# Feed-forward of a transformer layer: the chosen path's mask is read back from DRAM by broadcasting loads instead of being spread by TensorE products

## The reference, cut to what matters

```python
x_mixed = _mix(x, mix_kernel)                       # each row with its two neighbours
h = jnp.einsum('bsd,pdm->bspm', x_mixed, W1) + b1   # 9 paths, 64 hidden values each
stacked_paths = jnp.einsum('bspm,pmd->bspd', h, W2) + b2
scores = jnp.tanh(x_mixed @ Wo1 + bo1) @ Wo2 + bo2
idx = jnp.argmax(scores, axis=-1)
weights = jax.nn.one_hot(idx, P, dtype=stacked_paths.dtype)
collapsed = jnp.einsum('bspd,bsp->bsd', stacked_paths, weights)
return _layernorm(x + collapsed, gamma, beta)       # and x + this, normalised once more
```

## Time and profile before

| | |
|---|---|
| median of 3 runs | 1554.53 us (1553.85 to 1555.71) |
| the profiled execution | 1557.27 us, of which the span of the trace is 1555.6 us |
| feed-forward stage in the trace | from 1181.6 us to the end |
| busy over the whole span | PE 94%, DVE 71%, ACT 62%, POOL 29% |
| granted TensorE clock over the span | 0.97 of full speed |

### The profile page before, as it was taken

One profiled execution on the slowest core, in us unless ns is written; L12 is line 12 of the kernel. 1 busy time (PEld: TensorE's weight loads), 2 busy tenths in 40 slices (PEclk: granted clock), 3 DMA queues, 4 the chain that ended last, 5 costly groups with the idle time before them and its releaser, 6 DMA issues. The chain is left out here.

```text
span 1555.6 us, 25379 instructions
## 1 busy us (share of the span) xinstructions
PE 1458.1 (94%) x8282; PEld 661.4 (43%) x8282; DVE 1104.5 (71%) x2645; ACT 957.7 (62%) x2103; POOL 445.2 (29%) x565
## 2 busy tenths in 40 slices
PE   5979978999999999999999999999988999999995
PEld 3645641333333333333333333333323656666664
DVE  3212239788888888888888888888733788788775
ACT  3635630777777777777777777777775455555432
POOL 5423430211113313213224124124234152222212
PEclk9989985999999999999999999999999999999997
DMA  4887864032364483383383373473632821110001
GB/s 121 267 272 259 270 222 99 26 97 61 101 149 82 118 167 88 111 163 98 110 148 116 118 134 108 126 138 92 118 45 64 151 68 55 55 48 20 28 27 41
DMA packets 166753, 178.19 MB, mean 115 GB/s; under 512 B 26397, under 2 KB 135784, under 8 KB 166632
## 3 DMA queue, kind: packets, MB, share of 16 engines
q1 hardware_dynamic: 166632, 176.70, 44.0%
HBM read 109.79 MB, written 66.06 MB: 113 GB/s over the span
## 5 line engine op out<-in xcount | busy, mean ns | idle before, releaser
L761 ACT ACTIVATE a_probs<-a_ps_s 128x512 f32<-128x512 f32 (+3 forms) x1536 | 648.1, 501 | 232.1 <-PE a_ps_s L934 228.5
L789 DVE CUSTOM_DVE_ANT_0 h_space<-a_ps_m,a_causal 128x640 f32<-128x640 f32 (+5 forms) x768 | 652.5, 888 | 121.1 <-PE a_ps_m L857 107.4
L934 PE MATMUL a_ps_s<-s_qs,s_ks 99*128 99x512 bf16 (+3 forms) x1536 | 406.0, 329 | 6.3 <-ACT a_probs L761 4.5
L857 PE MATMUL a_ps_m<-s_ks,s_qs 96*128 96x512 bf16 (+3 forms) x1536 | 385.9, 338 | 22.5 <-DVE a_mx L789 8.0
L716 POOL TENSOR_SCALAR_AFFINE_SELECT a_probs<-a_probs 128x512 f32<-128x512 f32 x256 | 163.2, 637 | 662.6 <-ACT a_probs L761 662.6
L892 PE MATMUL a_ps_o<-a_probs,s_vq 128*32 128x512 f32 (+3 forms) x3072 | 328.1, 498 | 5.7 <-POOL a_probs L716 3.7
L934 PEld LDWEIGHTS a_ps_s<-s_qs,s_ks 99*128 99x128 bf16 x1536 | 137.2, 97 | 331.0 <-ACT a_probs L761 241.9
L857 PEld LDWEIGHTS a_ps_m<-s_ks,s_qs 96*128 96x128 bf16 x1536 | 130.0, 99 | 201.9 <-DVE a_mx L789 69.3
L226 DVE TENSOR_TENSOR p_rest<-p_ps_qk,h_space 128x512 f32<-128x512 f32 x64 | 44.3, 692 | 154.8 <-ACT h_space L251 154.8
L1403 PE MATMUL f_ps_o<-f_w,f_hm 128*128 128x256 f32 (+1 forms) x640 | 151.1, 384 | 0.9 <-DVE f_y L1310 0.9
L1403 PEld LDWEIGHTS f_ps_o<-f_w,f_hm 128*128 128x128 f32 (+1 forms) x640 | 121.4, 192 | 27.4 <-issue 8.4
(11 more groups left out here) (124 smaller groups left out, 1213.6 us busy)
## 6 DMA issues: line engine op xcount, KB each, us to landing
qk_parts<-h_space SPq DMA_DIRECT2D x64, 384.0 KB, 2.9
s_qs<-qk_parts SPq DMA_DIRECT2D x192, 128.0 KB, 2.8
s_ks<-qk_parts SPq DMA_DIRECT2D x192, 128.0 KB, 2.8
v_rows<-h_space SPq DMA_DIRECT2D x16, 896.0 KB, 5.4
s_vq<-v_rows SPq DMA_DIRECT2D x32, 448.0 KB, 4.4
f_x_in<-in_L_attn_x_dram SPq DMA_DIRECT2D x16, 512.0 KB, 6.2
heads_out<-a_o_sb SPq DMA_DIRECT2D x128, 64.0 KB
f_x_in<-in_L_attn_x_dram SPq DMA_DIRECT2D x8, 1024.0 KB, 9.0
```

The lines of the kernel that those rows point to most:

```text
L761: act.activation(probs[:, st % PB, h, 0:width], ps_s[:, n % BANKS, 0:width], ACT.Exp, scale=SCALE).then_inc(exps[h % 2], 1)
L789: taken = dve.tensor_tensor_reduce(out=shown[:, i % 2, k * CHUNK:k * CHUNK + width], in0=row, in1=causal[:, SEQ - width:SEQ], scale=1.0, s ...
L857: last = pe.matmul(out, qs[0:TROWS, j, h, q], ks[0:TROWS, j, h, s:s + wide], start=k == 0, stop=mask is None)
L934: pe.matmul(ps_s[:, n % BANKS, 0:width], ks[0:MROWS, j, h, kt * P:(kt + 1) * P], qs[0:MROWS, j, h, q0:q0 + width], start=True, stop=True)\
```

## The change

The mask is no longer spread by TensorE. ACT copies the transposed pick to SBUF as before (now 9 partitions only), issues a DMA that stores it in a DRAM scratch `pick_rows` (9 KB), does the other copy and `end(n - 2)`, then waits for the store and for the masked products of the turn before (`load_masks`), and issues two DMAs that read the scratch back into `f_pmask`: for d = 0 and 1, rows d, d + 2, ... of the pick, repeated over 64 partitions each (320 KB and 256 KB, in pieces of 1 KB). The hidden values are kept at once in `f_hm`, where DVE multiplies them in place by `f_pmask` once both loads have landed; both inputs of these five products are now in SBUF. The bank of the mask products goes to the hidden products (three banks, HB = 3). The output products of a turn stand together, and PE waits for the masked values only ahead of `output(n - 1, ., 0)` in the next turn. Two constants on POOL go away.

```diff
-        hid = sb("f_hid", [P, MC, CHUNK], F32)
+        opt = sb("f_opt", [P, CHUNK], F32)
+        pmask = sb("f_pmask", [P, MC, CHUNK], BF16)
-        pick_t = sb("f_pick_t", [P, CHUNK], BF16)
+        pick_t = sb("f_pick_t", [PATHS, CHUNK], BF16)
+        pick_rows = nc.dram_tensor("pick_rows", (PATHS, CHUNK), BF16).ap()
...
-        mask_banks = [ps_h[:, 0, :], ps_h[:, 1, :], ps_k[:, :], ps_h[:, 1, :], ps_k[:, :]]
...
+                def load_masks(n):
+
+                    act.wait_ge(pick_stored, 16 * (n + 1))
+                    if not (isinstance(n, int) and n == 0):
+                        act.wait_ge(hm_done, MC * n)
+                    act.sem_inc(act_turn, 1)
+                    for d in range(2):
+                        paths = pick_rows[d:PATHS:2, :].rearrange("m (o s) -> o m s", o=1)
+                        act.dma_start(pmask[d * DM:(d + 1) * DM, 0:MC - d, :],
+                                      paths.broadcast_to((DM, MC - d, CHUNK))).then_inc(mask_loaded, 16)
...
-                            act.activation(hid[:, m, :], ps_h[:, (m + 1) % 2, :], ACT.Identity,
+                            act.activation(hm[:, c, m, :], ps_h[:, (m + 1) % HB, :], ACT.Identity,
...
                         act.wait_ge(pick_made, n + 1)
-                        act.activation(pick_t[0:PATHS, :], ps_pick[0:PATHS, :], ACT.Copy).then_inc(pick_kept, 1)
...
+                        act.activation(pick_t[:, :], ps_pick[0:PATHS, :], ACT.Copy).then_inc(pick_kept, 1)
+                        act.wait_ge(pick_kept, 2 * n + 1)
+                        if not (isinstance(n, int) and n == 0):
+                            act.wait_ge(mask_loaded, MASK_DMAS * n)
+                        act.sem_inc(act_turn, 1)
+                        act.dma_start(pick_rows, pick_t[:, :]).then_inc(pick_stored, 16)
                         act.activation(hm[DM:X2, c, LAST, :], ps_pick[0:PATHS, :], ACT.Copy).then_inc(pick_kept, 1)
                         if not (isinstance(b, int) and b == 0):
                             end(n - 2, c)
+                        load_masks(n)
                         if c == 0 and not last:
                             normalize(b + 1, 1 - e, 0)
...
-                    dve.wait_ge(k_made, MC * n + i + 1)
+                    dve.wait_ge(mask_loaded, MASK_DMAS * (n + 1))
                     dve.wait_ge(h_kept, (MC + 1) * (n + 1))
-                    dve.tensor_tensor(hm[0:rows, c, i, :], mask_banks[i][0:rows, :], hid[0:rows, i, :], ALU.mult)\
+                    dve.tensor_tensor(hm[0:rows, c, i, :], hm[0:rows, c, i, :], pmask[0:rows, i, :], ALU.mult)\
...
                         if before:
 
                             pe.wait_ge(pick_kept, 2 * n)
+                            pe.wait_ge(hm_done, MC * n)
                             output(n - 1, 1 - c, 0)
...
                         if before:
-                            output(n - 1, 1 - c, 1)
-                        pe.wait_ge(pick_kept, 2 * n + 1)
-                        pe.wait_ge(h_kept, (MC + 1) * (n + 1))
-                        for i in range(MC):
-
-                            if i >= 3:
-                                pe.wait_ge(hm_done, MC * n + i - 1)
-                            pe.matmul(mask_banks[i], widen[:, 2 * i:2 * i + 2, :].rearrange("p q m -> p (q m)"),
-                                      pick_t[:, :], start=True, stop=True).then_inc(k_made, 1)
-                            if i in (2, 4) and before:
-                                output(n - 1, 1 - c, 1 + i // 2)
+                            for t in range(1, CT):
+                                output(n - 1, 1 - c, t)
```

More of the change, by code:

```diff
@@ L962, in feed_stage @@
         X2 = DM + PATHS
+        HB = 3
+        MASK_DMAS = 16 * 2
         ones = sb("f_ones", [P, P], F32)
@@ L1027, in feed_stage @@
         pick_kept = sem("f_pick_kept")
-        k_made = sem("f_k_made")
+        pick_stored = sem("f_pick_stored")
+        mask_loaded = sem("f_mask_loaded")
         hm_done = sem("f_hm_done")
@@ L1208, in keep_hidden @@
                             act.wait_ge(h_made, MC * n + m + 2)
[L1209 removed]
+                            act.activation(hm[:, c, m, :], ps_h[:, (m + 1) % HB, :], ACT.Identity,
                                            bias=bias[:, m:m + 1]).then_inc(h_kept, 1)
[L1212 removed]
+                        if not (isinstance(n, int) and n == 0):
+                            act.wait_ge(sc_made, n)
+                        if not (isinstance(n, int) and n < 2):
+                            act.wait_ge(o_made, 2 * (n - 1))
                         act.wait_ge(h_made, MC * n + 1)
[L1214 removed]
+                        act.activation(opt[DM:P, :], ps_h[DM:P, 0, :], ACT.Tanh,
                                        bias=bias[DM:P, LAST:MC]).then_inc(h_kept, 1)
[L1216 removed]
+                        act.activation(hm[0:DM, c, LAST, :], ps_h[0:DM, 0, :], ACT.Identity,
                                        bias=bias[0:DM, LAST:MC]).then_inc(h_kept, 1)
@@ L1416, in hidden @@
                             m = LAST if i == 0 else i - 1
-                            if i >= 2:
-                                pe.wait_ge(h_kept, (MC + 1) * n + i)
-                            if i < 2 and before:
-                                pe.wait_ge(hm_done, MC * (n - 1) + (1, 4)[i])
+                            if i >= HB:
+                                pe.wait_ge(h_kept, (MC + 1) * n + i - HB + 2)
+                            elif before:
+                                pe.wait_ge(h_kept, (MC + 1) * n - (1, 0, 2)[i])
                             for k in range(KC):
-                                ins = pe.matmul(ps_h[:, i % 2, :],
+                                ins = pe.matmul(ps_h[:, i % HB, :],
                                                 w1_sb[:, k, 2 * m:2 * m + 2, :].rearrange("d p m -> d (p m)"),
```

23 lines of the change are left out of this document (7 added, 16 removed).

## The result

The change made the kernel slower: 1569.71 us median of 4 runs (1566.80 to 1572.03) against 1555.12 of before (1553.85 to 1557.20); the ratio is 1.0092, 95% interval 1.0070 to 1.0113. The profiled execution after took 1566.8 us, the fastest of the four, with a span of 1565.1 us against 1555.6 before: 9.5 us more. The traces explain these 9.5; the rest of the difference of the medians lies in executions that have no trace.

The account below looks back on a forecast made before the run. PE bounds the kernel before; after the change a ring of waits would, at 44.0 us a pair against 43.72. Ring +2.0, first turns +3.4 and back edge +1.3 sum to +6.7 on 1554.5: 1561 us, range 1546 to 1584.

Parts of the forecast that it names:

- the scalings ahead of the loads: On ACT, the four scalings of end(n - 2) hold back the mask loads by 2.0 us a turn.
- the ring: Waits from one turn's masked products to the next, through DVE, POOL, ACT and mask loads: 16.5 + T, 22.0 us a turn.
- PE's work, 39.9 us a pair: PE's time for two feed-forward turns without the mask products, 39.9 us instead of 43.7.
- T: Landing time of the two mask loads, counted from the issue of the first; taken as 5.5 us.
- the rival of the early landing: Mask loads land with T under 4.9; DVE bounds through POOL's add_beta, 42.0 us a pair, 1547 us; chance 0.24.
- That ACT issues the loads well before the scalings end: Sign of being wrong, on ACT: the mask loads would leave well before the scalings end; no size given.
- I charge nothing: DVE's masked products and POOL's add_beta, which block each other, would miss each other in the even turn: cost nothing.
- The store of the pick hides.: On ACT, the store's 2.0 us landing is covered by 0.6 us of copying and 2.0 of scaling before the loads.
- First turns +3.4: In the first turns the mask comes one round trip later: 11.1 us against 6.6, less 1.09 PE saves; +3.4 once.
- Back edge +1.3: At the loop's back edge DVE stands 3.17 us for instructions; 1.9 reached the pair before, all on the ring: +1.3.
- The lower granted clock where PE stands: Sign of being wrong: a lower granted clock on PE where it now stands waiting; no size given.
- one of its rivals: Mask loads into 64 partitions run at about half rate: T 6.7, 1578 us, or T 6.3, 1572 us; chance 0.24.

Follow-up runs that it names:

- first experiment: The changed kernel with a mask of all ones: no store of the pick, no mask loads, no wait for them; 1528.58 us, ratio 0.9819 to the kernel before.
- the last experiment: The changed kernel with early pick, early mask loads, residual's inputs in two parts, and POOL's odd-turn addition behind the masked products; 1545.76 us, ratio 0.9921.

## Why the prediction came out as it did

It said slower, 1561 us in a range of 1546 to 1584. The direction and the range held; the difference was forecast at 6.7 us and came out at 9.5 in the profiled executions and 14.6 in the medians. Two of its terms were wrong, in opposite directions: the scalings ahead of the loads were priced at 2.0 us a turn and cost 0.3, and the store was put at nothing and cost some 9 us.

The direction was luck. The prediction has the ring lose 0.28 us a pair; it gained 1.3. With 42.4 us a pair and its other terms its own sum gives 7 x -1.3 + 4.7 = -4.4, which is 1550 us and faster. And with the store really hidden, as without the residual's inputs, the medians are 0.7 us apart: no change, to which it gave 0.14. Slower it became in turns 2 to 5, where the prediction had nothing but the first round trip.

- **PE's work, 39.9 us a pair.** Right: 39.6 a pair over turns 6 to 13 where nothing else binds (first experiment).
- **The ring, 22.0 us a turn.** The failed term is "the four scalings, 2.08 in the row, 2.0 until ACT can issue the next thing": measured 0.35 in turn 10 and 0.26 in turn 9, since ACT issues DMAs while its scalings still run. In the even turn the others held. From the second `add_x1` (1414.18) to the scaling that `f_nb_b` releases (1425.63) it is 11.45, forecast 11.5; T is 5.7 and 5.6, forecast 5.5; products 3.09, forecast 3.0, with 3.81 where POOL runs beside them. The ring closes on these: 3.81 + 12.73 + 0.26 + 5.57 = 22.4 for turn 8 to 9 and 3.09 + 11.45 + 0.35 + 5.68 = 20.6 for turn 9 to 10, and the starts of masked products, 1388.86, 1411.16, 1431.66, are 22.3 and 20.5 us apart. The pair of turns 6 and 7 takes 42.4, not 44.0. That is the time which the rival of the early landing gave (42.0), reached by a shorter ring and not by a shorter T. That ACT issues the loads well before the scalings end was among the prediction's own signs of being wrong, and it came.
- **The 22.3.** In the odd turn `f_nb_b` ends 1.2 us later than the terms give (hence 12.73 for 11.45). POOL's power takes 1.97 us there and `f_nb_b` 0.43, while they took 1.01 and 0.20 before (the second of them at 1412.40): beside DVE's mix, POOL is blocked too. POOL of the kernel after, in turn 9:

```profile
1402.73 1.97 POOL L1106 TENSOR_TENSOR f_rs_b<-f_ve_b,f_half 128x4 f32<-128x4 f32 x1 [5.87 <-DVE f_ve_b L1281]
1404.78 0.43 POOL L1125 TENSOR_TENSOR f_nb_b<-f_nm_b,f_rs_b 128x4 f32<-128x4 f32 x1
```

  "I charge nothing" was nearly right for DVE's products, by a wait that kept the two apart: 3.09 or 3.10 us in ten of the 16 turns, 3.5 to 4.0 in turns 4, 8, 10 and 12, 4.3 in turn 0 and 5.6 in turn 3.
- **"The store of the pick hides."** Right in the steady state (1.4 us in the odd turns of the experiment with the loads first, against 2.1 and more until the loads leave), wrong in turns 1 and 2, where it takes 7.8. This is the term that was put at nothing, and its price is the largest of all: the experiment without the inputs takes 11.0 us out of turns 2 to 5 and 9.0 of the 9.5 us of difference. The loads into 16 partitions stood in the earlier trace rows; the prediction read a rate off them and did not ask what the store, issued at 1215.17 between them, would find.
- **First turns +3.4.** As a round trip that is exposed once it is about right, but it shows at the end, +3.3 us in the changed kernel and 4.7 without the inputs, since the last turn has no later work of the ring to cover it (PE stands 6.56 us there). **Back edge +1.3:** the pair with it takes 45.1 us against 42.4 after, 45.66 against 43.72 before: +0.7.
- **The lower granted clock where PE stands**, named as a sign of error, came: 0.72 over 12 us in turns 2 and 4, and for shorter in turns 1, 3 and 9 (0.76 over 1203 to 1210 and 1261 to 1268, 0.79 over 1390 to 1398). Turn 3 had its drop before the change too (0.66 over 1263 to 1268), behind a wait of 2.48 us.

By "DMA: Bandwidth & Descriptors" of the Trainium skill, section "Queues, rings and completion order", the queues of SP and ACT run on the same 16 DMA engines, and the write that signals a transfer's completion lands only after every earlier write from that engine, across its queues. The trace agrees with the outcome: 1.4 us for the store alone and 7.8 with 1 MB and eight loads of 128 KB issued from 1205.9 to 1213.5. But the rule on the completion write is not what made the store late, since its data moved only from 1220.9 on. Why ACT's queue got no packet through for 5.7 us beside SP's no run here shows.

What stays open: why the other executions of the changed kernel take 2 to 5 us more than the profiled one. It was not traced.

## What to carry to other kernels

Before a small transfer is put into a chain that an engine waits for, go through all transfers that are in flight at that moment in every stage, the first turns above all, and not through the steady state alone; here 9 KB cost 9 us. With the pick and its loads issued early as well, the big transfers issued later made the kernel 1.4% faster than before instead of 0.9% slower. When a wait goes away, look at what it kept apart: the products met POOL's addition as soon as the mask came in time. When an edit delays one engine, look at what other engines issue behind it: POOL's late addition also put off SP's loads by some 20 us. And an edit that is good in the steady state can hold up something that stands behind it in an engine's order elsewhere, as the last experiment did: 1.6 us won, 13.5 lost.

## What the hardware showed that was not expected

- ACT issued a DMA 0.26 to 0.35 us behind the start of an activation, with three more of 0.6 us still to run. The issue stood behind the semaphore for which the first activation waited (1400.00 behind 1399.74 with the pick early), but not behind the activations' ends.
- A store of 9 KB to DRAM released the next DMA 1.4 us after its issue on quiet DMA engines, and after 7.8 us behind 1 MB and eight loads into 16 partitions of another queue; for 5.7 of these none of its packets moved.
- The loads into 64 partitions: 131 KB in two landed in 2.6 us each (median), 590 KB in two in 4.8. As an estimate from these, (590 - 131) kB in 2.2 us, that is 209 GB/s. The Trainium skill, "SBUF — State Buffer", "Door 1: The DMA port swizzle", measured 196 GB/s for a load of 1 MB into partitions 0 to 63, and gives about 218 GB/s without the fixed cost. The slope here has no fixed cost in it, so 218 is the one to compare; the runs agree roughly. By the 196 the prediction had T at 6.3 us, as one of its rivals; it was 5.7 and 5.6.
- DVE and POOL block each other both ways: POOL's power took 1.97 us instead of 1.01 beside the mix, DVE's five products 5.29 instead of 3.09 beside `add_beta`.
- After PE had stood for 3.7 and 3.1 us its granted clock was 0.72 over 12 us, which cost 2.8 and 2.7 us on the same 30 products. After 2.4 us of standing (turn 9) it was 0.79 over 8 us. Waits of 0.2 to 1.4 us in turns 6 to 8 and 10 to 13 left it at 1.00.
